# Second layer of a graph network on one core: one comparison of two tensors per group on VectorE instead of two comparisons with a number per partition

## What is computed

```python
# first layer
h = x @ W1 + b1
e = jnp.concatenate([h[dst], h[src] - h[dst]], axis=-1)
m = jax.nn.relu(jax.nn.relu(e @ W2 + b2) @ W3 + b3)
x = layernorm(x + relu(segment_max(m, dst)))
# second layer (the dst and src of edge_index swap roles: rows are gathered at dst, summed at src)
msgs = edge_weight[:, None] * x[dst]
x = layernorm(x + segment_sum(msgs, src) @ WL.T + bL)
```

## Time and profile before

| | us |
|---|---|
| Median of 3 runs | 2429.19 (2429.13 to 2429.34) |
| The profiled execution | 2430.71 |
| Its span, first to last instruction | 2428.9 |

### The profile page before, as it was taken

One profiled execution on the slowest core, in us unless ns is written; L12 is line 12 of the kernel. 1 busy time (PEld: TensorE's weight loads), 2 busy tenths in 40 slices (PEclk: granted clock), 3 DMA queues, 4 the chain that ended last, 5 costly groups with the idle time before them and its releaser, 6 DMA issues.

```text
span 2428.9 us, 59455 instructions
## 1 busy us (share of the span) xinstructions
PE 1894.0 (78%) x15384; PEld 1651.2 (68%) x15384; DVE 1540.5 (63%) x4339; ACT 998.8 (41%) x3021; POOL 1284.7 (53%) x1324
## 2 busy tenths in 40 slices
PE   5657777777777777767777449989999999699995
PEld 5645555555555555555565338888888888699995
DVE  5556667666676666676666944445445444388887
ACT  3412333332233333233333244555555555466665
POOL 6366566666666666666666434666666666500001
PEclk8779899999999999999999659999999999899998
DMA  4445555555555555555555356777777777699996
GB/s 130 127 122 149 148 156 152 151 155 151 155 150 153 155 152 152 153 149 146 149 148 150 102 176 216 236 230 239 242 232 242 237 237 239 215 284 290 288 284 202
DMA packets 533247, 452.12 MB, mean 186 GB/s; under 512 B 59036, under 2 KB 498296, under 8 KB 533153
## 3 DMA queue, kind: packets, MB, share of 16 engines
q1 hardware_dynamic: 374544, 260.16, 37.6%
q0 software_dynamic: 53312, 138.17, 18.3%
q10 hardware_dynamic: 105296, 52.84, 7.4%
HBM read 291.57 MB, written 159.37 MB: 186 GB/s over the span
## 4 chain that ended last, share of the span: by engine, by line
PE 48%; issue 15%; DVE 13%; another core or an unknown queue 11%; ACT 3%; DMA 3%; SPq 2%; DVEq 2%; POOL 1%; ACTq 1%; POOLq 0%
PE t_ps L1553 7%; PE z_ps L1553 7%; PE m_ps L1553 7%; PE z_ps L1478 4%; DVE run L1069 4%; PE m_ps L1465 3%; PE t_ps L1487 3%; PE m_ps L1466 3%; PE m_ps L1579 2%; PE z_ps L1579 2%; DVE whole L1047 2%; PE t_ps L1579 2%; DMA whole<-tab 2%; DVE oh L968 1%
## 5 line engine op out<-in xcount | busy, mean ns | idle before, releaser
L448 POOL DMA_INDIRECT whole<-q_tab,src_ti x784 | 763.1, 973 | 482.7 <-remote 245.6
L471 POOL DMA_INDIRECT tab<-whole,row_at x392 | 405.2, 1034 | 276.5 <-issue 84.4
L1198 DVE TENSOR_SCALAR whole<-row_bc,node_id 128x768 f32<-128x768 uint8 x392 | 230.7, 630 | 329.2 <-DMA row_bc<-rel_tab 290.6
L700 ACT ACTIVATE m<-m_ps,bias 128x512 f32<-128x512 f32 x196 | 134.7, 687 | 645.6 <-remote 605.1
L1465 PE MATMUL m_ps<-ident,whole 128*128 128x128 f32 x1568 | 324.3, 290 | 33.2 <-issue 21.6
L1466 PE MATMUL m_ps<-oh,win 128*128 128x128 f32 x1568 | 315.8, 284 | 0.3 <-issue 0.3
L1465 PEld LDWEIGHTS m_ps<-ident,whole 128*128 128x128 f32 x1568 | 258.7, 206 | 75.0 <-issue 63.7
L996 DVE TENSOR_TENSOR scratch<-s_ps,blk_oh 128x196 f32<-128x196 f32 x196 | 70.6, 360 | 297.8 <-remote 284.2
L1466 PEld LDWEIGHTS m_ps<-oh,win 128*128 128x128 f32 x1568 | 252.0, 202 | 1.0 <-issue 1.0
L1069 DVE TENSOR_TENSOR_SCAN run<-row_bc,run,z_ps 128x512 f32<-128x512 uint8 x195 | 248.5, 1274 | 2.0 <-ACT z_ps L705 1.8
L1478 PE MATMUL z_ps<-m,w 128*128 128x512 f32 x392 | 236.2, 687 | 0.0
(11 more groups left out here) (295 smaller groups left out, 3603.0 us busy)
## 6 DMA issues: line engine op xcount, KB each, us to landing
whole<-tab SPq DMA_DIRECT2D x409, 194.0 KB
win<-p_tab SPq DMA_DIRECT2D x784, 64.0 KB
seg_tab<-run_e ACTq DMA_DIRECT2D x196, 256.0 KB
win<-xw_tab SPq DMA_DIRECT2D x392, 128.0 KB
row_bc<-seg_row_tab SPq DMA_DIRECT2D x196, 128.0 KB
row_bc<-rel_tab SPq DMA_DIRECT2D x196, 96.0 KB
tab<-zeros SPq DMA_DIRECT2D x67, 200.0 KB
whole<-q_tab,src_ti POOLq DMA_INDIRECT x784
```

Source lines behind the costliest of these rows:

```text
L448: pool.indirect_dma_start(qg[:, g % RING, j, :], None, q_tab[:, :], IOA(ap=src_ti[:, t:t + 1], axis=0)).then_inc(q_ld[g % RING], 16)
L471: pool.indirect_dma_start(tab[:, :], IOA(ap=row_at[0:FR, k:k + 1], axis=0), fat[0:FR, k % RR, :], None).then_inc(fat_st[k // GK % RS], 16)
L700: nc.scalar.activation(m1[:, s, :], m1_ps[:, s, :], ACT.Relu, bias=bias12[:]).then_inc(relu1, 1)
L1198: last = V.tensor_scalar(pick[:, s, j, :], row_bc[:, s, 0:GK * SLOTS], node_id[:, j:j + 1], None, ALU.is_equal)
```

## The change

The two comparisons of a group, each of 768 uint8 slot numbers with a number per partition, become one comparison of two tensors with 1536 results: the slot numbers repeated for both tiles, and both numbers of the partition repeated over the 768 slots. The results, their places and the waits stay as they are; pick_done is raised by the one instruction.

```diff
@@ -1194,9 +1194,8 @@
                 dve.wait_ge(row_ld[s], 16 * (ROWS0[s] + i_of(i, r, RING) + 1))
                 if old(i, r - UN, RING):
                     dve.wait_ge(fat_ps, GK * (grp(i, r - UN, RING) + 1))
-                for j in range(CK):
-                    last = V.tensor_scalar(pick[:, s, j, :], row_bc[:, s, 0:GK * SLOTS], node_id[:, j:j + 1], None, ALU.is_equal)
-                last.then_inc(pick_done, 1)
+                V.tensor_tensor(pick[:, s, :, :], row_bc[:, s, 0:GK * SLOTS].unsqueeze(1).to_broadcast([P, CK, GK * SLOTS]),
+                                node_id[:, 0:CK].unsqueeze(2).to_broadcast([P, CK, GK * SLOTS]), ALU.is_equal).then_inc(pick_done, 1)
```

## The result

| | us |
|---|---|
| Changed kernel, median of 4 runs | 2473.81 (2473.12 to 2475.06) |
| Before, median of the 4 runs beside it | 2429.16 (2428.37 to 2429.34) |
| Ratio | 1.0182, 95% interval 1.0170 to 1.0194 |
| Span of the profiled execution, before and after | 2428.9 and 2471.4 |

The change makes the kernel 44.6 us slower. The measured time lies outside the range of 2427 to 2434.5 us, and the forecast of no difference is wrong too. The number of rival A, 2470 us, is 4 us away.

What follows compares the result with a forecast made beforehand. TensorE was taken to bound the fat-row stage, with VectorE working ahead. Terms of 0 us plus 0.3 us for late landings gave 2431.0 us profiled, 2429.5 us as median of the runs (chance 0.86); range 2427 to 2434.5 us.

Steps and rivals of the forecast that it cites:

- rival A: GpSimd's scatters are held by the new two-input comparison, half of it per group: +41 us, 2470 us; chance 0.06.
- the 0 us for GpSimd's scatters: In the fat-row stage, scatters freed of stretching gain 0.26 us a pair, which counts 0 us as GpSimd doesn't set the pace.
- The cost of the comparison: On VectorE, one comparison takes 1.75 us instead of 1.14 us: 0.6 us more per group, 118 us in all, hidden.
- rival B: The uint8 input is read at the scan's pace, 3.4 us a comparison, and VectorE becomes the bound: +107 us, 2536 us; chance 0.03.
- VectorE's slack and the later comparison: In the fat-row stage VectorE works ahead of TensorE, so its longer time and later comparison ends cost 0 us.
- the comparison would end only 0.6 and 1.2 us nearer to its matmuls: First and second comparison of a pair end that much later, none behind its matmuls on TensorE.
- "GpSimd isn't the pace": In the fat-row stage, TensorE doesn't start later after a longer series of four scatters, so GpSimd's time counts 0 us.
- rival C: GpSimd is relieved of stretching and does set the pace: 0.26 us a pair, -24 us, 2405 us; chance 0.05.
- The two starts of TensorE that were compared: TensorE goes on 0.45 us after a long scatter series, 1.03 us after a short one; taken as evidence against rival C.
- the steady 409 to 425 and 665 to 689 ns of the two-tensor comparisons: Existing VectorE comparisons keep these times although GpSimd works beside them; held against rival A.
- The stretching of the present comparisons: On VectorE, comparisons with a number per partition take 605 to 855 ns beside scatters; read as the trace's only kind of interference.

Runs made afterwards that it cites:

- time-only run: The kernel before with a one-input reduction of 430 constant elements on VectorE ahead of pick_done: ratio 1.0005, 2400.2 us.
- one-input run: The kernel before with its two comparisons in the form that also writes out a sum: ratio 1.0017, 2402.2 against 2398.1 us.
- last chip: Chip of the last series, which reran the kernel before, 2143.75 us, and the unaltered change beside it, 2253.6 us, ratio 1.0507.
- third series: Series on another chip that ran the unaltered change against the kernel before: 2254.3 against 2144.2 us, ratio 1.052.

## Why the prediction was wrong, point by point

- **The step that failed** is the 0 us for GpSimd's scatters. The sum let them get shorter, from 1.034 to 0.97 us, and had no term for a hold. They became 1.42 us, four of them with their steps 6.9 us, over the 6.5 us of a pair; that is the loss, +44.6 us here and +110 us where before is quicker.
- **The cost of the comparison: right.** 1.75 us forecast, 1.754 measured. VectorE's busy time rose by 1668.1 - 1540.5 = 128 us, 118 forecast. The uint8 input cost nothing (rival B falls).
- **VectorE's slack and the later comparison: right in cost.** The time-only run, 1.0005, and the one-input run, 1.0017 with more time still, show the 0 us of the sum. The forecast that the comparison would end only 0.6 and 1.2 us nearer to its matmuls isn't met: in the changed kernel it ends 0.4 us ahead of the group's first fat matmul in the middle case, as the key copy in front of it on VectorE now waits for a scatter to land. The waits of TensorE in those 600 us don't name the comparison (on the last chip they do with 2.3 of 450 us), so this follows from the hold and adds next to nothing.
- **"GpSimd isn't the pace" (rows 6): right for before, but not for the reason given.** Freeing the scatters to 0.98 us gained nothing on either chip (rival C falls). The two starts of TensorE that were compared, at 1708.04 and 1785.55 us, are single last records of a group, ahead of which the program has no wait; a scatter could have delayed neither. The step from there to "0 us" for the changed kernel held only while its scatters stayed as they were.
- **What was held against rival A was the wrong sign.** I read the steady 409 to 425 and 665 to 689 ns of the two-tensor comparisons as a sign that they and the scatters share nothing. The hold has one side: the comparison of two tensors runs on (1745 to 1820 ns), the scatter stands still. The scatters' durations by what runs beside them would have shown it, and they were in the trace of before:

```profile
1706.13 1.15 DVE L1198 TENSOR_SCALAR whole<-row_bc,node_id 128x768 f32<-128x768 uint8 x2
1706.43 1.16 POOL L471 DMA_INDIRECT tab<-whole,row_at  x1 [0.30 <-issue]
```

  The scatter of 1706.43 us ends at 1707.59; the comparison in which it began started at 1706.13, and its first instruction of about 0.61 us ended at 1706.74, 0.85 us earlier. 86 scatters from 1600 to 2000 us ran inside the present comparisons 0.12 us after their start, and about two thirds of them have the same end, 0.84 to 0.86 us behind the instruction in which they began; a comparison of 0.6 us is only too short to hold one for long. With 1.75 us in place of 0.61, that distance gives a scatter of up to 1.75 + 0.85 = 2.6 us, which is what came (2.55).
- **The stretching of the present comparisons** (605 to 855 ns), which I took for the mark of sharing, is the wrong side to look at: what VectorE loses is hidden in its slack, what the scatter loses isn't once GpSimd has none left.
- **Rival A's mechanism and price were right, its chance wasn't.** It had 0.06. Its sum used half a comparison for each of two groups, 1.75 us a pair, where the scatters grew by 4 x (1.42 - 0.97) = 1.8 us; 6.9 us a pair against 7.03 measured, and +41 us against +44.6. Half a comparison was an assumption that no row showed; that it came out so near is in part luck. The rule of the Trainium skill that was weighed there (SBUF — State Buffer, Who interferes with whom), contention of an instruction with two SBUF inputs with a GpSimd instruction that reads SBUF, would have given the result. The runs agree with it: scatters of 0.98 us with one input, of 1.14 us with two at nearly the same VectorE time.
- The comparison of line 1047, of two SBUF tensors and 0.68 us, could not have told: of the 389 gathers from 600 to 1200 us, none starts inside it, so its steady time says nothing on what happens to a scatter that does.

What stays open: why the pace of before is 5.8 us a pair on one chip and 6.5 in the first measurement, at the same granted clock of 1.00 in the stage. TensorE's idle time is most of the difference, 54 of 600 us against 8 of 450, or 0.5 of 0.7 us a pair, and the trace names no one for it. Transfers that land late can't be all of it: about 33 of the 54 us lie inside a group, most ahead of its last two records, where the program has no wait, and on the last chip no such piece is there.

## What to carry to other kernels

Before you replace a comparison with a number per partition by one of two tensors in SBUF, look at what GpSimd issues meanwhile. Group its instructions by the VectorE instruction in which they start, and see whether their ends keep a fixed distance from its end. If they do, the length of the single VectorE instruction is what counts, not its total; cut it, or use a form that doesn't hold, here the one that writes out its sum, at its price in VectorE's time. And the slack of an engine off the path is a number that differs with the chip: GpSimd's 4 x (1.034 + 0.30) = 5.3 us of before left 1.2 us a pair in the first measurement and 0.4 us on the last chip, so state from what length on that engine becomes the pace.

## What the runs showed of the hardware that I had not expected

- A GpSimd scatter that starts inside a comparison, but neither with its start nor in its last 0.13 us, ends 0.84 to 0.86 us after it, whether that is the present form of 0.6 us or one of two tensors of 0.95 or 1.75 us; it isn't slowed, it waits. Two comparisons issued back to back still let it go between them in nearly all cases.
- The form of a comparison that writes out its sum takes 1.008 us for 768 elements against 0.615 us, and held none of the 153 scatters that began inside it.
- The same kernel took 2429 us in the first measurement, and 2398, 2144 and 2143 us on the three chips of the later series; the same change cost 1.8% in the first, 5.2% in the third series and 5.1% in the last.
